# Table loads ahead of the crossing, and the accumulating transfer between rotation and spread

## The reference

```python
q, k, v = (cproj(Wq), cproj(Wk), cproj(Wv))            # x @ W, complex, per head
qr, kr = q * phase, k * phase                          # phase = cos + i sin of t * omega
E = exp(clip(-mu * |t - t'|, MIN_EXP, 0))              # decay per head
s = einsum('bihd,bjhd->bhij', qr, conj(kr)).real       # scores
qn, kn = squared norms of q and k
V = sigma_sq/(2 mu) * (1 - E*E) + eta_sq + gamma_sq
maha = maximum(qn + E*E*kn - 2 E s, 0) / V
logits = coef * log1p(maha / nu) - 0.5 * DH * log(V)   # masked to be causal
out = softmax(logits) @ v ;  x = x + out @ Wo
```

## Time and profile before

| | |
|---|---|
| median of three runs | 1673.64 us (1672.57 to 1674.62) |
| profiled execution | 1672.11 us, of which the span is 1670.2 us |
| granted TensorE clock | 0.998 of 2.4 GHz |
| busy: PE, DVE, ACT, POOL | 1616.2, 1457.7, 1443.9, 1116.1 us |
| DMA queues: from SyncE, from GpSimd | 98.07 MB, 31.46 MB |

### The profile page before, as it was taken

How to read it: one execution, slowest core, us unless ns; L and a number is a source line. 1 busy time by engine, 2 the same in 40 slices (tenths; PEclk the granted TensorE clock), 3 DMA queues, 4 the chain that set the end, 5 groups by cost and what they waited for, 6 DMA issues and landing times. The chain is left out here.

```text
span 1670.2 us, 30882 instructions
## 1 busy us (share of the span) xinstructions
PE 1616.2 (97%) x9690; PEld 1228.9 (74%) x9690; DVE 1457.7 (87%) x3020; ACT 1443.9 (86%) x2909; POOL 1116.1 (67%) x1074
## 2 busy tenths in 40 slices
PE   5999988999999999999999999999999999899998
PEld 4787865777777777777777777777777776677876
DVE  6878888899899989999998998999899889967665
ACT  6677778999999999999999999999999999775765
POOL 3554556778668767776877787777777677245555
PEclk9999999999999999999999999999999999999999
DMA  6000023444444444444443544354454433000000
GB/s 179 1 1 1 1 92 80 89 118 91 112 96 108 100 100 107 94 113 92 111 101 89 123 95 103 80 124 101 99 115 88 111 83 75 22 7 7 14 13 13
DMA packets 67761, 131.49 MB, mean 79 GB/s; under 512 B 10128, under 2 KB 27792, under 8 KB 67600
## 3 DMA queue, kind: packets, MB, share of 16 engines
q1 hardware_dynamic: 50320, 98.07, 22.9%
q0 software_dynamic: 17280, 31.46, 10.9%
HBM read 17.95 MB, written 5.24 MB: 14 GB/s over the span
## 5 line engine op out<-in xcount | busy, mean ns | idle before, releaser
L1501 POOL TENSOR_TENSOR early<-early 128x1024 f32<-128x1024 f32 x127 | 303.3, 2388 | 305.2 <-PE pS L1192 164.4
L661 POOL TENSOR_TENSOR hid_lo_d<-hid_d,hid_hi_d 128x512 fp32r<-128x512 f32 x176 | 231.4, 1315 | 218.8 <-ACT hid_hi_d L566 213.2
L1192 PE MATMUL pS<-early 128*128 128x128 f32 (+3 forms) x1024 | 297.6, 433 | 0.4 <-PEq L115 0.4
L1377 ACT ACTIVATE early<-early,nmax 128x128 f32<-128x128 f32 (+3 forms) x512 | 281.0, 558 | 13.0 <-DVE nmax L1588 13.0
L1393 ACT ACTIVATE early<-early,qnorm 128x128 f32<-128x128 f32 (+3 forms) x512 | 246.7, 553 | 48.5 <-DVE early L1601 47.6
L1597 DVE SCALAR_TENSOR_TENSOR pS<-pS,ek 128x1280 f32<-128x1280 f32 x128 | 191.7, 1498 | 73.6 <-PE pS L1192 72.2
L1192 PEld LDWEIGHTS pS<-early 128*128 128x128 f32 x1024 | 164.7, 191 | 96.1 <-issue 61.4
L1510 POOL TENSOR_TENSOR ek<-early 128x128 f32<-128x128 f32 (+3 forms) x256 | 215.8, 871 | 3.0 <-ACT early L1385 2.5
L1510 POOL TENSOR_TENSOR ek<-decay,early 128x128 f32<-128x128 f32 (+3 forms) x256 | 214.7, 866 | 0.0
L1406 ACT ACTIVATE early<-early,params 128x512 f32<-128x512 f32 (+1 forms) x256 | 196.5, 816 | 0.0
L1234 PE MATMUL pS<-ident,early 128*128 128x128 f32 x1280 | 182.0, 278 | 6.9 <-DVE early L1601 4.5
(11 more groups left out here) (395 smaller groups left out, 3836.5 us busy)
## 6 DMA issues: line engine op xcount, KB each, us to landing
early<-early SPq DMA_DIRECT2D x263, 256.0 KB, 3.5
x_sb<-weighed POOLq DMA_DIRECT2D x120, 256.0 KB, 4.2
early<-trig_d SPq DMA_DIRECT2D x64, 64.0 KB, 2.4
trig_d<-early SPq DMA_DIRECT2D x3, 1024.0 KB, 7.0
early<-in_w SPq DMA_DIRECT2D x3, 704.0 KB, 8.6
x_sb<-in_x SPq DMA_DIRECT2D x4, 512.0 KB, 8.3
early<-in_wqk SPq DMA_DIRECT2D x16, 128.0 KB, 3.4
cos<-trig_d SPq DMA_DIRECT2D x32, 64.0 KB, 2.6
```

The lines of the kernel that those rows point to most:

```text
L661: g.tensor_tensor(hid_lo[:, par], hid[:, par], hid_hi[:, par].bitcast(F32), ALU.subtract).then_inc(lo_done, 1)
L1192: last = pe.matmul(s.pS[:, span(I)], rot[:, I * P:(I + 1) * P], rot[:, N:N + (I + 1) * P], start=True, stop=True)
L1377: last = a.activation(z[:, span(I)], z[:, span(I)], ACT.Exp, bias=nmax[:, I:I + 1], scale=-1.0, accum_out=rsum[:, r % 4, I:I + 1])
L1501: g.tensor_tensor(rot[:], by_cos[:], crossed[:], ALU.add).then_inc(S["rot_done"], 1)
```

## The change

On SyncE the table loads move ahead of the crossing of their step (its wait for the rotation before stays in front), and they are divided: four of the eight trigonometry loads in each of two steps (1 and 2 for the odd head, 6 and 7 for the even one), and one expansion per step, the largest tile first (steps 3 to 5 and 8 to 11). On GpSimd the accumulating transfer moves from the end of the step to between rotation and spread, and it is that of the pair four steps back, no longer three. `weighed` gets two buffers, each with its own semaphore, and `val_even` goes from three buffers to two, so that ScalarE's copy waits for the weighing two steps back.

```diff
@@ -1060,3 +1060,3 @@
         q_turned = s.dist[:, 2 * N:SW].rearrange("p (k d) -> p k d", k=2)
-        weighed = sb("weighed", [P, TILES, P])
+        weighed = [sb(f"weighed{k}", [P, TILES, P]) for k in range(2)]
         ek = sb("ek", [P, SW])
@@ -1064,3 +1064,3 @@
 
-        val_even = [sb(f"val_even{k}", [P, N]) for k in range(3)]
+        val_even = [sb(f"val_even{k}", [P, N]) for k in range(2)]
         val_odd = [sb(f"val_odd{b}", [P, N]) for b in range(B)]
@@ -1073,2 +1073,3 @@
         expanded = (S["expanded0"], S["expanded1"])
+        acc_done = (S["acc_done0"], S["acc_done1"])
         block = ctx.enter_context(nc.Block())
@@ -1123,3 +1124,5 @@
         FRONT, EXP, HALF, LOW, SQUARE, LN, MASK = (1, 2), (2, 3), (3, 6), (4, 7), (3, 5), (4, 6), (6, 7)
-        WEIGHTS, TRIG, EXPAND = (1, 5), (1, 9), (3, 8)
+        WEIGHTS = (1, 5)
+        TRIG_ODD, TRIG_EVEN = {1: (0, 1), 2: (2, 3)}, {6: (0, 1), 7: (2, 3)}
+        EXPAND_ODD, EXPAND_EVEN = {3: 2, 4: 1, 5: 0}, {8: 3, 9: 2, 10: 1, 11: 0}
 
@@ -1148,3 +1151,3 @@
 
-            def load_trig(h):
+            def load_trig(h, quarters):
                 par = h % 2
@@ -1152,8 +1155,8 @@
                 apart(sp, S["sp_passed"])
-                for q, table in enumerate((1, 2, 2, 1)):
+                for q in quarters:
                     rows = slice(q * DH // 2, (q + 1) * DH // 2)
                     sp.dma_start(cos[par][rows, :], s.trig_d[0, h]).then_inc(trig_in[par], 16)
-                    sp.dma_start(sin[par][rows, :], s.trig_d[table, h]).then_inc(trig_in[par], 16)
+                    sp.dma_start(sin[par][rows, :], s.trig_d[(1, 2, 2, 1)[q], h]).then_inc(trig_in[par], 16)
 
-            def expand(h):
+            def expand(h, I):
 
@@ -1163,4 +1166,3 @@
                 wait(sp, S["t_done"], 2 * (h - 1) * B)
-                for I in range(TILES - par):
-                    sp.dma_start(decay[par][:, span(I)], far(h)[:, near(I)]).then_inc(expanded[par], 16)
+                sp.dma_start(decay[par][:, span(I)], far(h)[:, near(I)]).then_inc(expanded[par], 16)
 
@@ -1168,5 +1170,14 @@
                 c = r + 2
+                n = i * 16 + c
                 if live(i, c):
-                    n = i * 16 + c
                     wait(sp, S["rot_done"], n)
+                if building(WEIGHTS, i, r):
+                    load_weights(building(WEIGHTS, i, r))
+                if isinstance(i, int):
+                    for h, trig, expanding in ((i * 2 + 1, TRIG_ODD, EXPAND_ODD), (i * 2 + 2, TRIG_EVEN, EXPAND_EVEN)):
+                        if h < H and r in trig:
+                            load_trig(h, trig[r])
+                        if h < H and r in expanding:
+                            expand(h, expanding[r])
+                if live(i, c):
                     apart(sp, S["sp_passed"])
@@ -1175,8 +1186,2 @@
                     sp.dma_start(crossed[DH:P, :], by_sin[0:DH, :]).then_inc(S["crossed_in"], 16)
-                if building(WEIGHTS, i, r):
-                    load_weights(building(WEIGHTS, i, r))
-                if building(TRIG, i, r):
-                    load_trig(building(TRIG, i, r))
-                if building(EXPAND, i, r):
-                    expand(building(EXPAND, i, r))
 
@@ -1307,3 +1312,3 @@
                 wait(pe, S["val_done"], values_made(i, r))
-                val = val_even[r % B % 3] if parity(r) == 0 else val_odd[r % B]
+                val = val_even[r % B % 2] if parity(r) == 0 else val_odd[r % B]
                 turned = probT[r % 2]
@@ -1415,5 +1420,5 @@
                 a.wait_ge(S["v_done"], values_made(i, r))
-                if live(i, r - 3):
-                    wait(a, S["av_done"], i * 16 + r - 2)
-                for h, val in enumerate((val_even[r % B % 3], val_odd[r % B])):
+                if live(i, r - 2):
+                    wait(a, S["av_done"], i * 16 + r - 1)
+                for h, val in enumerate((val_even[r % B % 2], val_odd[r % B])):
                     last = a.activation(val[:].rearrange("p (j d) -> p j d", j=TILES),
@@ -1523,3 +1528,3 @@
                 xb = s.x_sb[:, b * TILES:(b + 1) * TILES, :]
-                g.dma_start(xb, weighed[:], accum_op=ALU.add).then_inc(S["acc_done"], 16)
+                g.dma_start(xb, weighed[n % 2][:], accum_op=ALU.add).then_inc(acc_done[n % 2], 16)
 
@@ -1530,6 +1535,7 @@
                         rotate(i, r + 1)
+                if live(i, r - 4) and n - 4 < (H - 1) * B:
+                    accumulate(i, r - 4)
+                if live(i, r + 1):
                     spread(i, r + 1)
                     query_norms(i, r + 1)
-                if live(i, r - 3) and n - 3 < (H - 1) * B:
-                    accumulate(i, r - 3)
                 if i == 0 and r == -1:
@@ -1617,3 +1623,3 @@
                 if n >= (H - 1) * B:
-                    v.wait_ge(S["acc_done"], 16 * (n - B + 1))
+                    v.wait_ge(acc_done[n % 2], 16 * ((n - B) // 2 + 1))
                     for I in range(TILES):
@@ -1624,4 +1630,4 @@
                     return
-                wait(v, S["acc_done"], 16 * n)
-                v.tensor_tensor(weighed[:], s.p7.rearrange("p (c d) -> p c d", c=TILES),
+                wait(v, acc_done[n % 2], 16 * (n // 2))
+                v.tensor_tensor(weighed[n % 2][:], s.p7.rearrange("p (c d) -> p c d", c=TILES),
                                 rinv[:, r % 4, :].unsqueeze(2).broadcast_to([P, TILES, P]), ALU.mult).then_inc(S["y_done"], 1)
...
```

More of the change, by code:

```diff
@@ L1847, in program @@
                  "ek_done s_done w_done t_done relu_done ln_done zred_done exp_done v_done "
-                 "y_done qt_done val_done tr_done trc_done av_done rinv_done acc_done stat_done dve_passed pool_passed sp_passed "
+                 "y_done qt_done val_done tr_done trc_done av_done rinv_done acc_done0 acc_done1 stat_done dve_passed pool_passed sp_passed "
                  "late_stat late_mv late_var late_ln late_root late_rstd late_step late_xn late_xt late_hi late_lo mv_done expanded0 expanded1")
```

## The result

The changed kernel takes 1702.53 us (median of four runs, 1702.49 to 1703.39) against 1674.13 us of the kernel before, measured beside it: ratio 1.0173 [1.0158, 1.0189], slower by 28 us. Forecast were 1679.5 us, range 1673 to 1688: the direction was right, the size was not. The profiled span grew from 1670.2 to 1700.6 us.

A forecast was written before the change was run, and what follows sets the result against it. TensorE, 97% busy, was taken as the bound. Profiled 1672.11 us, minus 10.0 surplus, plus 13.9 to 17.7 for late spread, middle +5.8, gave 1677.9; plus 1.5 for the median, 1679.5 us, range 1673 to 1688.

The forecast's parts named there:

- Spread waits for the issue: GpSimd: the 0.88 us transfer issue delays spread, which ends 9.89 us after the scores; even steps lose nothing.
- VectorE's wait: VectorE's wait for the transfer before writing weighed, 1.9 us in five cases, goes away with two buffers.
- What a late end costs: Odd heads: spread ending late against VectorE's peaks costs 13.9 to 17.7 us, including about 0.5 in the last head.
- The rule on the port pair: VectorE and GpSimd lock a shared SBUF port for whole instructions; some 11 us over the kernel, left out.
- The surplus of 10 us is won: Odd-head stretches: the 10.0 us above TensorE's own step lengths all go, through moved transfer and table loads.
- Rotations start 3.3 us into every odd step: GpSimd, odd steps: every crossing lands on time, so rotation starts 3.3 us in; later than 3.6 would refute it.
- a rival at 0.10 and 37 us: Odd steps: the accumulating transfer in flight makes every crossing late, +37 us, about 1711; chance 0.10.
- Values in two buffers, table loads: ScalarE's values copy costs 0, at worst 6 us; trigonometry loads in even heads cost up to 0.3 us per head.

The follow-up runs named there:

- the last experiment: Kernel with later transfer issue and earlier crossing, but all table loads behind their crossing as before the change: 1673.14 us, ratio 0.9993.
- the tiny transfer: Changed kernel with the accumulating transfer cut to 16 columns of one tile, its issue kept: 1715.38 us, ratio 1.0246.
- the gaps: Changed kernel with GpSimd waiting for its own piece after each of the first three of spread's four pieces: 1704.45 us, ratio 1.0174.
- the move undone: Changed kernel with the accumulating transfer issued at the end of GpSimd's step again, rest kept: 1673.32 us, ratio 0.9993.
- the old tables: Changed kernel with the table loads behind their crossing again, as before the change: 1700.14 us, ratio 1.0153.
- these eleven kernels: The kernel before, the changed one and the follow-up variants of both, from 1668.04 to 1715.38 us.

## Why the prediction was right in direction and wrong in size

- *Spread waits for the issue.* Right. Its end lies 9.92 us after the scores (forecast 9.89), even steps stay at 9.87, VectorE's wait of the earlier trace rows is gone (though not by the second buffer, as the last experiment shows).
- *What a late end costs.* Mis-sized. I took loss = end - 0.95 or 0.72 x (end - 0.64), 13.4 to 17.2 us over seven heads. Measured is end - 0.66, 0.80 and 0 in turn: 3.2 a head (two heads with the tiny transfer have 3.26 and 3.20, each with one late crossing in it), 22.4 us for seven. (The low end of my own range was too high besides: with an issue of 0.80 us the first line gives 1675, not 1677.) The rows came from a spread whose pieces leave VectorE room; behind a DMA issue they don't, as the gaps showed. The rule on the port pair that I set aside as no part of the sum (the Trainium skill, SBUF — State Buffer, "SBUF: two separate sides") was on the right track: VectorE was held up whole instructions at a time, here by spread's four in a row.
- *The surplus of 10 us is won.* Wrong, and the first of the two steps that failed. I read the earlier trace rows as a meeting with the accumulating transfer and the earlier trace rows as table loads behind a crossing. Both have a code packet 2.60 us after the issue. With the transfer nearly gone eight crossings stay late, with the move undone ten, and 6.2 of the 9.2 us in the seven heads follow late crossings. What I had right is VectorE's wait, some 2 us of the 10: the divided loads win it.
- *Rotations start 3.3 us into every odd step.* Wrong, the second and the larger: I put late crossings at nothing. They start at 3.86 in the mean, and 30 of 49 crossings are late. I had this as a rival at 0.10 and 37 us, with the right mechanism; it happens not in every step, but where a code packet has made the step before late.
- *Values in two buffers, table loads.* Costing them at nothing was right.

The sum for the seven heads: the surplus of 36.2 is 22.4 for the insertion, by the law, and 13.8 that are left for late crossings and what follows them (1.6 of it clock); less the old surplus of 9.2 that is +27.0, where I had +3.4 to +7.2. The split is an estimate, as the two act on each other: with the tiny transfer fewer late crossings cost more.

## What to carry to other kernels

Before a surplus is booked as won, look in the DMA records at what is in flight in the late and in the punctual case: the transfer you see issued nearby need not be the one that delays. A DMA that an engine issues between two of its operations costs twice where the chain is closed, once by its issue, and once because a delay moves it onto the transfer that starts the next round. And where a latency can't be removed, start it sooner: moving a short operation behind the one that feeds the crossing won 0.2 to 0.4%, here mostly because 2 to 4 crossings were late in place of 10. A second buffer takes no wait away if the transfer that empties it is issued as much later.

## What was not expected of the hardware

- TensorE's code loads compete with the kernel's transfers: a packet of 16 KB takes 0.9 us, and one that starts 2.5 to 3.1 us after a crossing's issue makes the 4.23 us of that crossing 5.0 to 5.7. Among the 49 counted steps of these eleven kernels every such crossing is late, and none is whose packet starts 3.48 us or more after the issue (4.2 to 4.6 us).
- GpSimd instructions behind a DMA issue run closer together than others (rows that overlap by 0.28 us in place of 0.03 to 0.05), and VectorE, with two inputs in SBUF, does not get in between: 2.55 us for a piece that takes 0.35 to 0.4 alone.
- Pauses of TensorE can cost more than their length: 1.54 us were followed by 1.6 us lost at the lower clock, and 3.67 us (granted clock 0.60 from 845.0 to 853.5) by 0.85 us lost in the transposes (2.36 in place of 1.51) and 1.4 in the weighing. It isn't every pause: with the tiny transfer five of six pauses of 3.25 to 3.67 us came with a fall of the clock, with the old tables none of five of 1.44 to 1.61 us.
